# A four-layer model step on one core: order of the row gathers, making of the tile table, and place of the late expert weights in a mixture-of-experts layer

## What is computed

```
h = relu(einsum('td,ndf->ntf', flat, shared_w1) + shared_b1[:, None, :])      # 2 shared experts, 512 -> 352
shared_out = einsum('ntf,nfd->td', h, shared_w2) + shared_b2.sum(0)
out = flat + shared_out
scores = sigmoid(flat @ centroids.T) + bias                                   # 16 routed experts
vals, idx = top_k(scores, 4)
gating = zeros_like(scores).at[arange(T)[:, None], idx].set(vals); gating /= clip(gating.sum(-1), 1e-08)
for w1, b1, w2, b2, g in the 16 routed experts:
    acc = acc + (relu(flat @ w1 + b1) @ w2 + b2) * g[:, None]
return out + acc
```

## Time and profile before

| | |
|---|---|
| median of three runs | 1342.42 us |
| the profiled execution: its own time | 1343.04 us |
| its span in the trace | 1341.2 us |
| TensorE matmul, busy | 1012.6 us (75%) |
| VectorE, ScalarE, GpSimd, busy | 713.0, 665.7, 563.5 us |
| mean granted TensorE clock | 0.915 of full speed |
| first and last transposes of the routed part begin | 412.28 and 838.73 us |

### The profile page before, as it was taken

The page is one execution under the profiler, slowest core; times in us unless marked ns, Lnnn a source line. Parts: engine busy times, 40 slices in busy tenths (PEclk is TensorE's granted clock), DMA queues, the critical chain, the costliest instruction groups (busy, mean ns, idle before and its releaser), DMA issues. The chain is left out here.

```text
span 1341.2 us, 27817 instructions
## 1 busy us (share of the span) xinstructions
PE 1012.6 (75%) x9405; PEld 569.2 (42%) x9406; DVE 713.0 (53%) x1717; ACT 665.7 (50%) x1064; POOL 563.5 (42%) x483
## 2 busy tenths in 40 slices
PE   4789999789985778899899998337787887888200
PEld 1465655556663556666566666211121111211000
DVE  6676655689872653222222222263545677765775
ACT  4555645445531654344344443246676676888200
POOL 0333321556751344455455554332223455454535
PEclk9899999899997889999899999778999889999755
DMA  6342323799925866656556655546546555556110
GB/s 245 123 144 96 125 76 127 175 203 225 203 76 166 276 146 120 110 96 108 117 103 110 103 105 106 122 136 116 135 115 130 127 137 137 148 121 128 67 37 2
DMA packets 187923, 172.50 MB, mean 129 GB/s; under 512 B 141730, under 2 KB 143074, under 8 KB 186914
## 3 DMA queue, kind: packets, MB, share of 16 engines
q1 hardware_dynamic: 161952, 117.19, 33.6%
q0 software_dynamic: 24576, 53.83, 20.4%
q10 hardware_dynamic: 1298, 0.20, 0.1%
HBM read 81.12 MB, written 65.23 MB: 109 GB/s over the span
## 5 line engine op out<-in xcount | busy, mean ns | idle before, releaser
L1758 ACT ACTIVATE sb_atp<-ps_atpS 128x1024 f32<-128x1024 f32 x256 | 249.3, 1025 | 94.7 <-PE ps_atpS L1590 93.1
L1360 PE MATMUL ps_shpY<-sb_rowt,sb_rohhl 128*128 (+1 forms) x711 | 173.9, 391 | 14.7 <-DVE sb_rohhl L1249 13.7
L1371 PEld LDWEIGHTS ps_shpH<-sb_roxT,sb_rowt 128*128 (+1 forms) x2844 | 170.2, 107 | 20.4 <-issue 2.2
L1371 PE MATMUL ps_shpH<-sb_roxT,sb_rowt 128*128 128x128 f16 (+1 forms) x2844 | 174.5, 221 | 0.7 <-DVE sb_roxT L1244 0.7
L1600 PE MATMUL ps_atpO<-sb_atp,sb_atv 128*17 128x512 f32 x1024 | 142.0, 628 | 0.8 <-ACT sb_atp L1758 0.8
L1590 PE MATMUL ps_atpS<-sb_atq,sb_atk 64*128 64x512 f16 x512 | 97.0, 397 | 41.9 <-DMA sb_atv<-vst 25.0
L1123 ACT ACTIVATE sb_roh<-ps_shpH,sb_rob 128x128 f32<-128x128 f32 (+1 forms) x237 | 68.7, 361 | 93.4 <-PE ps_shpH L1371 92.4
L1112 ACT ACTIVATE sb_roy<-ps_shpY,sb_roentry 128x512 f32<-128x512 f32 x79 | 54.2, 687 | 122.4 <-PE ps_shpY L1360 122.4
L1031 POOL DMA_INDIRECT x2a<-sb_roy,sb_roentry x40 | 63.4, 1586 | 111.2 <-ACT sb_roy L1112 111.2
L1360 PEld LDWEIGHTS ps_shpY<-sb_rowt,sb_rohhl 128*128 128x128 f16 (+1 forms) x711 | 67.9, 100 | 85.1 <-issue 22.9
L1024 POOL DMA_INDIRECT sb_roxg<-xn,sb_roentry x79 | 82.1, 1040 | 47.6 <-issue 22.5
(11 more groups left out here) (297 smaller groups left out, 1801.5 us busy)
## 6 DMA issues: line engine op xcount, KB each, us to landing
sb_rowt<-rw SPq DMA_DIRECT2D x15, 768.0 KB, 10.6
sb_rowt<-rw SPq DMA_DIRECT2D x15, 704.0 KB, 8.3
kst<-sb_kykp SPq DMA_DIRECT2D x16, 512.0 KB
qst<-sb_quqp SPq DMA_DIRECT2D x16, 512.0 KB, 4.0
vst<-sb_kyvt SPq DMA_DIRECT2D x16, 272.0 KB
sb_atv<-vst SPq DMA_DIRECT2D x32, 136.0 KB, 4.0
sb_stage<-ctxT SPq DMA_DIRECT2D x4, 1024.0 KB, 7.4
sb_shxin<-x SPq DMA_DIRECT2D x16, 256.0 KB
```

Of the source, the lines that this page charges most:

```text
L1360: last = e.matmul(pY[it.p][:, :], hhl[it.p][0:n, x, k * P:(k + 1) * P], weight(value, 2 * W1 + w + k * D, n, D), start=j == 0, stop=j == l ...
L1371: last = e.matmul(rpH[it.p][0:n, f * P:(f + 1) * P], weight(ex["up"], w + k * FF + f * P, P, n), rxT[it.p][:, x + k, :], start=j % (3 * KD ...
L1758: S.done(e.activation(pr[u % 4][:, :], pS[u % 2][:, :], ACT.Exp, scale=HD ** -0.5 / SA ** 2), "atexp")
```

## The change

The tile table is made with tiles on partitions: VectorE compares the running sums of tiles with each partition's number (a new constant `c_part`, loaded by SP), so that every operation has 16 columns (the comparison of counts 256), and TensorE turns the two resulting columns into rows with two matmuls against the identity. GpSimd's stream holds gather n, then scatter n - 5. SP waits for the lists and loads four entries ahead of that beat's store; it issues the weights of experts 7 to 13 each followed by two entry loads (4 to 11). The beats of the late splits and of the small pieces are later. ScalarE and TensorE wait for the table before their loops.

```diff
...
         e.dma_start(small["rb1"][:, :], a["rb1"]).then_inc(S.sem("rob1"), 16)
+        e.dma_start(small["part"][:, :], a["c_part"]).then_inc(S.sem("sh_part"), 16)
         for n in range(KEY_FIRST):
...
         gr = sb(mem, "shgr", [P, 1])
-        cnt = sb(mem, "shcnt", [P, NR])
+        cnt, limit, tiles, skip, past = (sb(mem, "sh" + n, [P, NR]) for n in ("cnt", "limit", "tiles", "skip", "past"))
+        sums = [sb(mem, f"shsums{i}", [P, NR]) for i in range(2)]
+        more = sb(mem, "shmore", [P, NR, NR])
+        which = sb(mem, "shwhich", [P, 2])
+        tabf = sb(mem, "shtabf", [P, 2], f16)
 
...
         early_beat = {5 + 2 * k: k for k in range(EARLY)}
-        late_beat = {n: beat for n, beat in zip(range(EARLY, direct), (1, 2, 3, 5, 6, 7, 9, 10))}
-        small_beats = (11, 12, 13, 14)
+        late_beat = {n: beat for n, beat in zip(range(EARLY, direct), (3, 4, 5, 7, 8, 9, 10, 12))}
+        small_beats = (12, 13, 14, 15)
 
...
                     S.wait_moved(e, "shxnout", It(NT // 2 - 1, p))
-                e.wait_ge(S.sem("shtable"), 1)
-                first_entries(0, 2)
+                e.wait_ge(S.sem("shtable"), 2)
+                first_entries(0, 4)
 
...
                 keys.store(e, KEY_LATE + it.n)
-            beats([(load, 0, 0, NT), (store, 7, 0, NT), (turn, 2, 0, NT), (early, -2, 0, LAST), (values_out, 2, 0, NT - KEY_LATE), (keys_out, 7, 0, NT - KEY_LATE),
-                   (lists_done, NT + 4, 0, 1)], -2, LAST - 1)
-            first_entries(2, FIRST)
+            beats([(lists_done, NT + 4, 0, 1), (load, 0, 0, NT), (store, 7, 0, NT), (turn, 2, 0, NT), (early, -2, 0, LAST), (values_out, 2, 0, NT - KEY_LATE), (keys_out, 7, 0, NT - KEY_LATE)], -2, LAST - 1)
             e.wait_ge(S.sem("shdown"), NT)
...
                 weights(n)
+                first_entries(min(2 * (n - EARLY) + 4, FIRST), min(2 * (n - EARLY) + 6, FIRST))
 
...
             pipeline(e, N2, [(entries, 0, FIRST, N2), (query_weights, 0, QBEAT, QBEAT + 1), (last_weights, 2, late_beat[direct - 2], late_beat[direct - 2] + 1),
-                             (small, 2, small_beats[0], small_beats[-1] + 1)])
+                             (small, 2, small_beats[0], small_beats[1]), (small, 2, small_beats[1], small_beats[-1] + 1)])
 
...
             beats([(low, 2, 0, NT), (root, 1, 0, NT), (scatter, 4, 0, NT)], 0, LAST)
-            for n in range(N2 + 4):
+            for n in range(N2 + 5):
                 if n < N2:
...
                         in_offset=bass.IndirectOffsetOnAxis(ap=rentry[:, n, 0:1], axis=0)), "rogather", it)
-                if n >= 4:
-                    it = It((n - 4) // 2, n % 2)
+                if n >= 5:
+                    it = It((n - 5) // 2, (n - 5) % 2)
                     S.wait(e, "roy", it)
...
                         out=R["x1" if it.p else "x2a"],
-                        out_offset=bass.IndirectOffsetOnAxis(ap=rentry[:, n - 4, 0:1], axis=0),
+                        out_offset=bass.IndirectOffsetOnAxis(ap=rentry[:, n - 5, 0:1], axis=0),
                         in_=y[it.p][:, :], in_offset=None, compute_op=ALU.add), "roadd", it)
...
                 S.done(e.activation(wt[:, q_at:q_at + QW], raw[:, q_raw:q_raw + QW], ACT.Copy, scale=SW), "roqhi")
+            e.wait_ge(S.sem("shtable"), 2)
             pipeline(e, N2, [(rchoose, 2), (rhidden, 2), (rout, 3), (query_high, 0, QBEAT + 4, QBEAT + 5)] + [late(n) for n in range(EARLY, direct)]
-                     + [(small, 0, small_beats[0], small_beats[-1] + 1)])
+                     + [(small, 0, small_beats[0], small_beats[1]), (small, 0, small_beats[1], small_beats[-1] + 1)])
 
...
             v.wait_ge(S.sem("sh_small"), 32)
+            v.wait_ge(S.sem("sh_part"), 16)
             line = Line(S, v, "shdve")
...
                 tail(v.scalar_tensor_tensor(cnt[:, :], K["iota"][:, :], -float(CAP), base[NT % 2][:, :], ALU.mult, ALU.add))
-                make_table(tail, v, mem, sb, "t2", NR, N2, cnt[:, :], K, K["tab2"][0:1, 0, :], K["tab2"][0:1, 1, :],
-                           None, None)
-                S.done(v.tensor_scalar(K["tab2"][0:1, 0, :], K["tab2"][0:1, 0, :], -1, NR - 1, ALU.mult, ALU.add), "shtable")
+                tail(v.tensor_scalar(limit[:, :], K["iota"][:, :], float(P), None, ALU.mult))
+                tail(v.tensor_tensor(more[:, :, :], bcast(cnt[:, 0:1], [(1, NR), (0, NR)]), bcast(limit[:, 0:1], [(0, NR), (1, NR)]), ALU.is_gt))
+                tail(v.tensor_reduce(tiles[:, :], more[:, :, :], AX.X, ALU.add))
+                tail(v.tensor_scalar(tiles[:, :], tiles[:, :], 1.0, None, ALU.max))
+                tail.go(v.tensor_scalar(skip[:, :], tiles[:, :], -1.0, float(CAP // P), ALU.mult, ALU.add))
+                last = tiles
+                for i, d in enumerate((1, 2, 4, 8)):
+                    cum = sums[i % 2]
+                    tail.go(v.tensor_copy(cum[:, 0:d], last[:, 0:d]))
+                    tail(v.tensor_tensor(cum[:, d:], last[:, d:], last[:, 0:NR - d], ALU.add))
+                    last = cum
+                tail(v.tensor_scalar(past[:, :], last[:, :], part[:, 0:1], None, ALU.is_le))
+                tail.go(v.tensor_reduce(which[:, 0:1], past[:, :], AX.X, ALU.add))
+                tail(v.tensor_tensor(past[:, :], past[:, :], skip[:, :], ALU.mult))
+                tail.go(v.tensor_scalar(which[:, 0:1], which[:, 0:1], float(NR - 1), None, ALU.min))
+                tail(v.tensor_reduce(which[:, 1:2], past[:, :], AX.X, ALU.add))
+                with nc.allow_low_precision(reason="whole numbers up to 336"):
+                    tail.go(v.tensor_scalar(tabf[:, 0:1], which[:, 0:1], -1.0, float(NR - 1), ALU.mult, ALU.add))
+                    S.done(v.tensor_tensor(tabf[:, 1:2], which[:, 1:2], part[:, 0:1], ALU.add), "shnumbers")
+
+            def numbers(it):
+                v.wait_ge(S.sem("shrow"), 1)
+                S.done(v.tensor_copy(K["tab2"][0:1, 0, :], pCw[0:1, 2 * NR:2 * NR + N2]), "shtable")
+                S.done(v.tensor_scalar(K["tab2"][0:1, 1, :], pCw[0:1, 2 * NR + N2:2 * NR + 2 * N2], float(P), None, ALU.mult), "shtable")
 
...
                 keys.low(v, KEY_LATE + it.n)
-            beats([(hidden, 6, 0, NT), (spread, 1, 0, NT), (finish, 7, 0, NT), (place, 4, 0, NT), (table, NT + 3, 0, 1),
+            beats([(hidden, 6, 0, NT), (spread, 1, 0, NT), (finish, 7, 0, NT), (place, 4, 0, NT), (table, NT + 3, 0, 1), (numbers, NT + 4, 0, 1),
                    (choose, 3, 0, NT), (norm, 1, 0, NT), (keys_squares, 2, 0, NT - KEY_LATE - 1), (early, 0, 0, LAST),
...
             pipeline(v, N2, [(evacuate, 0), (parts, 2), (query_low, 0, QBEAT + 4, QBEAT + 5)] + [late(n) for n in range(EARLY, direct)]
-                     + [(small, 0, small_beats[0], small_beats[-1] + 1)])
+                     + [(small, 0, small_beats[0], small_beats[1]), (small, 0, small_beats[1], small_beats[-1] + 1)])
 
...
                 S.done(last, "shdown")
-            beats([(up, 5, 0, NT), (route, 3, 0, NT), (count, 4, 0, NT), (down, 6, 0, NT)], 0, LAST)
+
+            def numbers(it):
+                e.wait_ge(S.sem("shnumbers"), 1)
+                for i in range(2):
+                    last = e.matmul(pCw[0:1, 2 * NR + i * N2:2 * NR + (i + 1) * N2], tabf[:, i:i + 1], K["ident"][:, 0:N2], start=True, stop=True)
+                S.done(last, "shrow")
+            beats([(up, 5, 0, NT), (numbers, NT + 4, 0, 1), (route, 3, 0, NT), (count, 4, 0, NT), (down, 6, 0, NT)], 0, LAST)
 
...
                 e.wait_ge(S.sem("ropl"), 2 * NP)
+            e.wait_ge(S.sem("shtable"), 2)
             pipeline(e, N2, [(ahead, 0, 1, N2 + 3), (turn, 0), (ready, 1, 0, direct), (small_ready, 1, direct, NR), (both, 1, 0, N2 + 2), (rup, 1)], unroll=8)
...
         "c_tok": (np.arange(NT)[None, :] * P + rowi[:, None]).astype(np.int32),
+        "c_part": rowi[:, None].astype(np.float32),
         "c_pad": (TOK + (np.arange(N1)[None, :] * P + rowi[:, None]) % (2 * P)).astype(np.float32),
...
```

More of the change, by code:

```diff
@@ L840, in phase_ffn @@
         h = sb(mem, "shh", [P, NS, FB * P])
+        part = sb(mem, "shpart", [P, 1])
         vt = [sb(mem, f"kyvt{i}", [P, NH * (HD + 1)]) for i in range(2)]
@@ L851, in phase_ffn @@
         near, far = Place(nc, nc.sbuf_base, first_slots), Place(nc, first_slots, nc.sbuf_top)
-        front = Front(nc, S, a, R, K, shared, {"b1r": b1r, "bias": bias, "rb1": rb1, "vt": vt, "sq": ksq, "ss": kss, "rr": krr}, far, near, pH, pY, pR)
+        front = Front(nc, S, a, R, K, shared, {"b1r": b1r, "bias": bias, "rb1": rb1, "part": part, "vt": vt, "sq": ksq, "ss": kss, "rr": krr}, far, near, pH, pY, pR)
         keys = front.keys
```

## The result

The changed kernel takes 1277.59 us, the median of four executions (1275.72 to 1281.58); the kernel before took 1342.66 beside it (four executions, 1337.81 to 1345.03). The ratio is 0.9524, 95% interval 0.9489 to 0.9559: 65 us or 4.8% faster. The forecast was 1276, which is 0.9505 of 1342.42.

A forecast was written before the change was run, and what follows sets the result against it. Gathers stuck behind scatters in GpSimd's stream were taken to bound the steady part, with a late start before it. Gains of 29.4 us (start) and 37.2 us (steady part) sum to 66.6, 1343.04 to 1276 us; range 1262 to 1304.

The forecast's parts named there:

- What bounded the kernel: Routed part, tiles 16 to 78: gathers queued behind scatters in GpSimd's stream hold beats at 5.14 us; TensorE needs 4.40.
- Part 1, the table: Start of the routed part: 21 small VectorE operations take 5.3 us, and tile 0's transposes start 5.8 us earlier.
- Part 2, entries and weights: Start of the routed part: expert 7's weights issued 13 us earlier, tile 16's transposes at 490.4, 29.4 us earlier.
- The choice of 8.35 us for tile 4's gather: Tile 4, in the weights' traffic: gather issue to use takes 8.35 us, as at tile 5 before, not the mean 4.64.
- I take 5.0 us for four beats: Tiles 4 to 8, in the weights' traffic: four beats of 5.0 us, putting tile 8's transposes at 447.
- no effect of the order: Rival, steady part: another hold keeps beats at 5.14 us, only the front's 29.4 us gained, 1314 us; chance 0.05.
- Part 3, the order: Tiles 16 to 78: gather ahead of one scatter more makes TensorE the bound, 281.7 us, gain 37.2.
- The edge I feared: Steady part: entry load plus gather take 7.8 us for two beats, 3.9 each, or 4.4 if the gather takes 5.56.
- The tail: After tile 78's transposes: the rest and the two later layers, behind a barrier, keep their length.
- The edge is missed: Rival, steady part: gathers and entry loads land later, beats about 4.8 us, gain 21.3, time 1292; chance 0.20.
- The start is given back: Rival, start: eight gathers in the weights' traffic don't overlap, 8.35 us a beat, front gain 5.6, time 1300; chance 0.12.
- Slower, the scatter's landing: Rival: ScalarE waits to write `y` until the scatter two tiles back lands; at 11 us landing, 1366 us; chance 0.04.

The follow-up runs named there:

- e1: The kernel before with GpSimd's new order alone (gather n, then scatter n - 5): 1305.22 us against 1361.66, ratio 0.9604.
- e2: The changed kernel with GpSimd's old order again (gather n, then scatter n - 4): 1349.28 us, ratio 0.9918 to the kernel before.
- e4: The kernel before with the new tile table alone: 1357.39 us, ratio 0.9966.
- e6: The changed kernel with SP's store of block 13 sent ahead of the wait for the lists and the entries: 1295.50 us, ratio 0.9518 to the kernel before.
- e7: The changed kernel with entry loads 4 to 11 all ahead of the weights: 1298.30 us, ratio 0.9547 to the kernel before.
- e5: The changed kernel unaltered, run again on another occasion: 1297.83 us, ratio 0.9531 to the kernel before.
- e9: The changed kernel with one scatter more behind (gather n, then scatter n - 6): 1297.75 us against 1346.75 for the kernel before, ratio 0.9624.
- e8: The changed kernel with expert 14's weights two beats later, behind entry loads 13 and 14: 1297.94 us, ratio 0.9537 to the kernel before.

## Why the prediction was right

The forecast was 1276 us, the measurement 1277.59, and the likeliest case is the one that came. By its steps:

**What bounded the kernel.** Right. A gather behind a scatter in GpSimd's stream set the beat; e1 and e2 move that one thing and the waits of the earlier trace rows go and come.

**Part 1, the table.** 5.3 us of VectorE forecast, 3.9 measured; C to T(0) 15.3 forecast (406.5 less 391.17), 15.1 measured. Alone (e4) it was worth 5.5 us at T(0) and 3.1 at T(16): the wait for the entry behind expert 14's weights, 4.54 us before, became 7.64.

**Part 2, entries and weights.** From T(0), in the forecast: 8.0 to T(3), 12.5 to T(4), 20 to T(8), 43.4 to T(16). Measured: 8.5, 13.5, 21.0, 45.7. Each term is 0.5 to 2.3 us short, and C to T(16) 103.7 in place of 99.2. Two sizes explain it, and the other beats gave a little back. The last store was put at 408 with nothing in front of it; block 13's went only at 405.27, behind four entry loads, and VectorE waited for it (e6: 3.9 us from C to T(16)). And tile 13's entry cost 8.4 us over two beats of 4.8, not 5: TensorE runs at the lower clock after the wait, so that tile 14 is late as well (2.9 us over 4.40, 0.6 of them for its rows). The choice of 8.35 us for tile 4's gather, over the mean of 4.64, was right (8.1).

The rule of the Trainium skill ("DMA: Bandwidth & Descriptors", Queues, rings and completion order), that descriptors of one queue are consumed in ring order on each DMA engine, agrees: entry 4, issued behind expert 7's weights, lands after 6.1 us, and after at most 3.3 us when the entries stand ahead (e7). Traffic on the same DMA engines would slow a small load as well, and no run here tells the two apart.

**Where the reasoning failed.** The step was "I take 5.0 us for four beats", justified by gathers that "start 0.9 after the transposes two tiles before". That start is the new order's doing. I booked it under Part 2 and gave the order nothing ahead of T(16). e2 has the table and SyncE's order and no new gather order: T(4) to T(8) 28.8, C to T(16) 115.8. So SyncE's order and the table bring 12.8 us of the 24.9 by themselves, and the order's share of the start is 9.5 to 12. My rival "no effect of the order" was therefore wrongly priced: not 1343.0 - 29.4 = 1314 but 0.9918 of 1342.7, 1332.

**Part 3, the order.** Forecast 281.7 us for 62 beats, measured 280.7. 62 x 4.40 = 272.8; the other 7.9 are 1.6 at tile 17 (expert 15's pieces), 4.4 at turns of the loop (0.5 at tile 18, 0.77 at each of five more), 1.7 at tiles 41 to 43 with the query load and one more turn, and 0.2 spread; I had 4.9 for turns and 4 for the rest. The edge I feared, entries and gathers sharing two beats, is where GpSimd's 45.7 us of wait are; it holds 4.40 us all the same.

**The tail.** I kept it, and it was 5.6 us shorter, which happens to make up for the start's shortfall. It is no gain of the change: over the twelve further runs, all with the same code behind B, B to the end is anything from 472.0 to 486.6 us, and 481.7 for the same kernel in e5. So the sum is right to 0.1% with some luck in it; 24.9 + 38.2 = 63.1 from C on is what the change is worth in these two traces, and the medians differ by 65.1.

**The rivals.** "The edge is missed": no, 4.53 us a beat and not 4.8. "The start is given back": only 4.5 us of it. "Slower, the scatter's landing": not here; but ScalarE did wait 0.7 to 2.6 us for a scatter in the weights' traffic, and e9 shows such waits one step further, at no cost in the steady part and with beats of 10.4 and 10.5 us in the start.

## What to carry to other kernels

When an in-order queue issues a transfer behind an instruction that waits for late data, count the stages between its issue and its use, and move it ahead by one; then check the buffer on the other side, for the next step may use up its margin (e9). When several edits share one stretch, price each alone and together, since here the gather order was worth 10 us in a stretch that I had credited to the weights' order. A small load may go ahead of a large one or behind it, but where the large one's reader is as late, the place only chooses who waits (e7, e8).

## What the runs showed of the hardware that I had not expected

- **Two turns of a long loop cost more than all the turns of the short one.** One turn of TensorE's loop of eight beats shows 0.6 us of "issue". A beat has 53 matmuls and as many weight loads, so sixteen beats are some 1700 instructions and more; a turn there shows 3.92 and 4.55 us, and the instruction queue moves 28 packets in 250 us in place of 3. The two long turns cost 10.5 us, the five short ones between T(18) and T(78) outside the query load 0.8 each. The Trainium skill ("Runtime: NRT & Kernel Launch", Instruction fetch mechanics) says that a taken branch to code that is no longer held forces a fetch before execution goes on, which agrees, and that TensorE holds 2048 instructions; it also speaks of a window of two pages of 256, but the loop of eight, some 850 instructions, turned without such a stall. Whether the loop of sixteen passes 2048 with its waits and register instructions, no row here counts.
- **The same code takes 472 to 487 us in the last phases** from one execution or occasion to the next, and the shared part ends 16 us apart. A part of 5 us can be read only from stages with a common start.
- **The turns of the loop had been mostly hidden.** Before, the transposes of even tiles show two waits of "issue", 1.3 us, in 320 us; with the gathers out of the way they show seven, 3.5 us, in 290.
